# A feature-interaction kernel: who multiplies and who splits in its opening, and the order of its first weight and input loads

## The chip, the cores and the metric

The kernel runs on one core of a Trainium2 chip. The metric is the device time of one execution in microseconds (us): 2739.86 is the median of three runs (2738.73 to 2740.82). Engines: TensorE (PE), VectorE (DVE), ScalarE (ACT), GpSimd (POOL) and SyncE (SP), which here only issues DMAs.

## What is computed

1024 samples have 39 fields with an embedding of 16 numbers each. Three layers multiply every pair of rows and mix the products with a matrix; a two-layer dense net runs over the same inputs, and one dot product sums all:

```python
inputs = emb[feature_ids] * feature_vals[:, :, None]        # (1024, 39, 16)
h = inputs
for i in range(3):                                          # 200 outputs each
    x = jnp.einsum('bhd,bmd->bhmd', h, inputs).reshape(B, -1, 16)
    x = jax.nn.relu(jnp.einsum('bcd,oc->bod', x, Ws[i]) + bs[i][None, :, None])
    if i != 2:
        h, direct = x[:, :100], x[:, 100:]
    else:
        direct = x
    finals.append(direct)
cin_result = jnp.sum(jnp.concatenate(finals, axis=1), axis=-1)
d = relu(relu(inputs.reshape(B, -1) @ dnn_W0.T + dnn_b0) @ dnn_W1.T + dnn_b1)
out = concat(cin_result, d) @ fc_W.T + fc_b + sum of the input biases
```

## The kernel before

**Chunks and steps.** A chunk is one of the 16 embedding positions for 128 samples, 128 chunks in all. Step i treats layer 0 of chunk i+1, layer 1 of chunk i and layer 2 of chunk i-1, in the order of ORDER: groups P0, D0, D1, P1, D2, D3, P2, D4, D5, P3, D6, ... D11. A group is up to four tiles of 128 products x 128 samples. P0 and P1 are layer 0, P2 and P3 with D0 to D5 layer 1, P4, P5 and D6 to D11 layer 2. Products of P groups are made by GpSimd (`product`, L534) in SBUF, those of D groups by VectorE (L1112) in PSUM. Each is split in a high part (ScalarE, `high`, L833, rounded to fp32r) and a low part, what is left (`low`: GpSimd L562, VectorE L1131). PE (`multiply`, L667) multiplies high with both parts of the weights and low with the high part. Each engine works through its own list in order and waits on semaphores.

**Between the layers.** `low_copy` (ScalarE) and `evacuate` (VectorE) finish a layer's sum, `take` (ScalarE) makes h, `turn` (PE) transposes it, `spread` (ScalarE, six copies) lays it out for the products of the next layer.

**Weights.** Layer 1's and 2's go from their input to a copy in DRAM by rows (`rows_of_weights`, L309, eight DMAs in four quarters), from there to SBUF (`load_weights`, L321, 13 DMAs), and are split in five PIECES each (1600, 1600, 1600, 800 and 600 columns): the high part by ScalarE (`split_weights`, L825), the low part by VectorE (L1096). W_NEEDED names the piece that PE waits for ahead of a group. Layer 2's pieces are split within step 1, after D4 to D8 (W2_AT).

**Inputs.** 39 gathers of GpSimd (L511) fetch the first 128 samples. `first_scale` multiplies them by their values, `turn` transposes them, `store_rows` stores them to `xs` in DRAM; from there `load_layer0` (L381, 12 small DMAs) brings a chunk's layer-0 operands and `load_block` (L397) the rows `xrep` for layers 1 and 2, in four blocks e = 1, 2, 0, 3: D0 and D1 need block 1, D2 and D3 block 2, P2 and P3 block 0, D4 and D5 block 3.

**The opening.** The first two chunks' layer-0 operands don't come through DRAM: `lay_out_pairs` (L1063) copies them in SBUF, PE transposes them to PSUM (`first_inputs`, L721), `first_layer0` (L1086) copies them to SBUF on VectorE, and GpSimd multiplies and splits them. SP's list from L443 on: store the first four positions, wait, load chunk 0's blocks, copy layer 2's rows, load chunk 2's layer-0 operands, chunk 1's blocks, layer 2's weights, store the other positions. After the opening come step 1 and loops over the rest.

## Time and profile before

| | |
|---|---|
| median of three runs | 2739.86 us |
| profiled execution | 2743.04 us, its span 2740.1 us |
| busy in the span | PE 96%, VectorE 84%, ScalarE 67%, GpSimd 85% |
| DMA | 359.96 MB, mean 131 GB/s |

The span runs from the first to the last instruction. The page has it in 40 slices of 68.5 us: PE is at 0 in the first, 5 in the second, and 9 in all others but the last. The opening therefore has to be read from the timelines of the single engines.

### The profile page before, as it was taken

Reading aid. Unit: us, or ns where it says so; the run is one execution under the profiler, and the core shown is the slowest. Engines: PE = TensorE matmul, PEld = TensorE weight load, DVE = VectorE, ACT = ScalarE, POOL = GpSimd, SP = SyncE. Lnnn points to the kernel's source line nnn. Section 1 sums busy time; section 2 is a strip of 40 time slices with the busy share of each in tenths; the row PEclk is TensorE's granted clock in tenths of the full one; section 3 lists DMA queues with packets and bytes.
Section 4 is the critical chain, followed back from the end, with each engine's and each line's share of the span. In section 5 each row is a group of like instructions: output and inputs, shape, how many; then the busy total and the mean of one; then the engine's idle time right before and its main releaser. Section 6 shows DMA issues by size and latency. Waiting matters only on the chain.

```text
span 2740.1 us, 68376 instructions
## 1 busy us (share of the span) xinstructions
PE 2636.3 (96%) x17806; PEld 2626.6 (96%) x17806; DVE 2290.3 (84%) x4610; ACT 1830.4 (67%) x4776; POOL 2318.8 (85%) x2168
## 2 busy tenths in 40 slices
PE   0599999999999999999999999999999999999998
PEld 0599999999999999999999999999999999999998
DVE  3688888888888888888888888888888888888884
ACT  0566776767667767676676767777677766766763
POOL 5799888988889888898889888898888988877763
PEclk9799999999999999999999999999999999999999
DMA  8854545445444464544545445454554445445441
GB/s 149 198 135 128 137 132 136 126 120 141 130 134 132 123 151 120 138 129 122 153 117 141 126 129 146 120 141 122 142 134 124 136 122 149 129 122 140 115 127 40
DMA packets 245650, 359.96 MB, mean 131 GB/s; under 512 B 68975, under 2 KB 163026, under 8 KB 245330
## 3 DMA queue, kind: packets, MB, share of 16 engines
q1 hardware_dynamic: 231394, 352.75, 47.1%
q0 software_dynamic: 10496, 2.88, 3.0%
q10 hardware_dynamic: 3568, 2.71, 0.3%
q14 instruction: 185, 1.52, 0.2%
q8 instruction: 7, 0.11, 0.0%
HBM read 354.24 MB, written 14.17 MB: 134 GB/s over the span
## 4 chain that ended last, share of the span: by engine, by line
PE 94%; POOL 2%; SPq 2%; DVE 1%; issue 1%; DMA 1%; ACT 0%; POOLq 0%; DVEq 0%; ACTq 0%
PE acc L664 60%; PE acc L665 28%; PE acc L689 3%; POOL raw L511 1%; PE hrep L700 1%; SPq L327 0%; SPq L317 0%; DVE W L1110 0%; PE acc L764 0%; PE acc L765 0%; PE acc L766 0%; DMA odd<-lin 0%; SPq L384 0%; PE hrep L786 0%; DMA raw<-table,idx 0%
## 5 line engine op out<-in xcount | busy, mean ns | idle before, releaser
L664 PE MATMUL acc<-W,xhi_d 128*128 128x400 f32 x5632 | 1729.8, 366 | 16.8 <-DVE xhi_d L1139 6.9
L665 PE MATMUL acc<-W,xlo_d 128*128 128x200 f32 x5632 | 1438.4, 255 | 0.0
L1136 DVE TENSOR_TENSOR xlo_d<-prod_d,xhi_d 128x512 fp32r<-128x512 f32 (+1 forms) x1536 | 984.9, 641 | 191.8 <-ACT xhi_d L846 117.9
L1128 DVE TENSOR_TENSOR prod_d<-hrep,xrep 128x512 f32<-128x512 f32 (+1 forms) x1536 | 1038.7, 676 | 105.6 <-issue 33.2
L664 PEld LDWEIGHTS acc<-W,xhi_d 128*128 128x128 f32 x5632 | 1060.4, 188 | 19.8 <-DVE xlo_d L1136 8.9
L665 PEld LDWEIGHTS acc<-W,xlo_d 128*128 128x128 f32 x5632 | 1078.7, 192 | 0.0
L846 ACT ACTIVATE xhi_d<-prod_d 128x512 fp32r<-128x512 f32 (+1 forms) x1536 | 884.1, 577 | 214.6 <-PE acc L665 197.8
L570 POOL TENSOR_TENSOR xlo_p<-prod_p,xhi_p 128x512 fp32r<-128x512 f32 (+1 forms) x768 | 920.8, 1199 | 125.4 <-ACT xhi_p L840 100.8
L664 PE MATMUL acc<-W,xhi_p 128*128 128x400 f32 x2816 | 879.5, 363 | 14.9 <-POOL xlo_p L570 14.9
L559 POOL TENSOR_TENSOR prod_p<-hrep_s,xrep 128x512 f32<-128x512 f32 x512 | 666.0, 1301 | 110.3 <-ACT hrep_s L883 76.4
L665 PE MATMUL acc<-W,xlo_p 128*128 128x200 f32 x2816 | 719.3, 255 | 0.0
L840 ACT ACTIVATE xhi_p<-prod_p 128x512 fp32r<-128x512 f32 (+1 forms) x768 | 473.2, 616 | 216.5 <-PE acc L665 116.1
L664 PEld LDWEIGHTS acc<-W,xhi_p 128*128 128x128 f32 x2816 | 531.9, 189 | 16.7 <-POOL xlo_p L570 13.5
L665 PEld LDWEIGHTS acc<-W,xlo_p 128*128 128x128 f32 x2816 | 539.6, 192 | 0.0
L511 POOL DMA_INDIRECT raw<-table,idx x328 | 319.8, 975 | 110.8 <-issue 90.2
L857 ACT ACTIVATE acc_lo<-acc 128x200 f32<-128x200 f32 x384 | 130.0, 339 | 290.8 <-PE acc L665 146.3
L559 POOL TENSOR_TENSOR prod_p<-l0x 128x512 f32<-128x512 f32 x128 | 165.0, 1289 | 19.8 <-DMA l0x<-xs 19.7
L1150 DVE SCALAR_TENSOR_TENSOR spent<-acc,fcw 128x100 f32<-128x100 f32 (+1 forms) x384 | 114.0, 297 | 49.1
L1146 DVE TENSOR_TENSOR acc<-acc,acc_lo 128x200 f32<-128x200 f32 x384 | 138.9, 362 | 6.8 <-ACT acc_lo L857 6.8
L551 POOL TENSOR_TENSOR prod_p<-l0x 128x384 f32<-128x384 f32 x128 | 130.9, 1023 | 3.5 <-POOL idx L506 1.7
L865 ACT ACTIVATE hbuf<-acc 128x96 f32<-128x96 f32 x256 | 63.3, 247 | 82.3 <-DVE spent L1150 80.6
L689 PE MATMUL acc<-W,xhi_d 128*128 128x400 f32 x256 | 93.3, 364 | 0.0
(105 smaller groups left out, 1208.6 us busy)
## 6 DMA issues: line engine op xcount, KB each, us to landing
xrep<-xs SPq DMA_DIRECT2D x384, 384.0 KB
xrep<-xs SPq DMA_DIRECT2D x384, 128.0 KB
xrep<-xs SPq DMA_DIRECT2D x128, 336.0 KB
l0x<-xs SPq DMA_DIRECT2D x504, 80.0 KB
l0x<-xs SPq DMA_DIRECT2D x252, 63.0 KB
l0x<-xs SPq DMA_DIRECT2D x630, 7.0 KB
xrep<-xs SPq DMA_DIRECT2D x128, 64.0 KB
l0x<-xs SPq DMA_DIRECT2D x126, 64.0 KB
```

The costliest lines, as they stand in the source:

```text
L511: nc.gpsimd.indirect_dma_start(out=raw[:, m * EMB_COLS:(m + 1) * EMB_COLS], out_offset=None, in_=table, in_offset=bass.IndirectOffsetOnAxi ...
L551: nc.gpsimd.tensor_tensor(to, l0x[:, KT[0]:L0_SLOTS - 1, :], l0x[:, a:a + count, :], ALU.mult)
L559: nc.gpsimd.tensor_tensor(to, one.unsqueeze(1).broadcast_to([P, count, P]), many, ALU.mult).then_inc(s_prod_p, 1)
L570: nc.gpsimd.tensor_tensor(xlo_p[:, slot, 0:cols], prod_p[:, slot, 0:cols], xhi_p[:, slot, 0:cols].bitcast(F32), ALU.subtract).then_inc(s_l ...
L664: pe.matmul(bank[:, 0:2 * OUTS], hi, w, start=first, stop=last, skip_group_check=True)
L665: return pe.matmul(bank[:, 0:OUTS], lo, w[:, 0:OUTS], start=False, stop=last, skip_group_check=True)
L689: mm = pe.matmul(bank[:, 0:2 * OUTS], hi, w, start=start, stop=end, skip_group_check=True)
L840: nc.scalar.activation(xhi_p[:, slot, 0:cols], prod_p[:, slot, 0:cols], ACT.Copy).then_inc(s_hi_p, 1)
L846: nc.scalar.activation(xhi_d[:, slot, 0:cols], prod_d[d_bank(i, g)][:, 0:cols], ACT.Copy).then_inc(s_hi_d, 1)
L1128: nc.vector.tensor_tensor(to, h, xrep[:, (par + layer - 1) % 2, a:a + count, :], ALU.mult).then_inc(s_prod_d, 1)
L1136: op = nc.vector.tensor_tensor(xlo_d[:, slot, 0:split], bank[:, 0:split], xhi_d[:, slot, 0:split].bitcast(F32), ALU.subtract)
L1146: nc.vector.tensor_tensor(bank[:, 0:OUTS], bank[:, 0:OUTS], acc_lo[:, layer, :], ALU.add).then_inc(s_acc[layer], 1)
```

## The change

- `first_layer0` becomes `first_products`: VectorE copies three of the ten turned tiles to SBUF and multiplies the other seven with them in PSUM. `first_high` (ScalarE) and `first_low` (VectorE) split them. PE's `first_inputs` turns ten tiles a chunk, not eleven, in another order and into banks named `first_banks`.
- GpSimd makes no product of the first two chunks' layer 0. It makes the low parts of layer 1's pieces 0 and 1 instead (semaphore `s_wlo_p`).
- ScalarE makes the high parts of layer 1's pieces 0 and 1 ahead of the first high copies, 2 and 3 between the two chunks, 4 after them.
- VectorE's scaling and transposition of positions 4 to 15 moves behind `evacuate(0, 1)`, GpSimd's gathers behind its first products of layer 1.
- SP copies the first quarter of layer 2's rows ahead of chunk 0's blocks, and issues `load_weights(2)` before chunk 1's blocks, not after.

```diff
+        W_OF_POOL = 2
-        W_NEEDED = [{("P", 0): 1},
-                    {("D", 0): 2, ("P", 2): 3, ("D", 2): 4, ("D", 4): 5, ("D", 5): 6},
-                    {("D", 6): 7, ("P", 4): 8, ("D", 8): 9, ("D", 10): 10, ("D", 11): 11}]
+        W_NEEDED = [{("P", 0): (s_wlo, 1)},
+                    {("D", 0): (s_wlo_p, 1), ("P", 2): (s_wlo_p, 2), ("D", 2): (s_wlo, 2), ("D", 4): (s_wlo, 3),
+                     ("D", 5): (s_wlo, 4)},
+                    {("D", 6): (s_wlo, 5), ("P", 4): (s_wlo, 6), ("D", 8): (s_wlo, 7), ("D", 10): (s_wlo, 8),
+                     ("D", 11): (s_wlo, 9)}]
+        first_banks = [(acc[1], prod_d[0], prod_d[1]), (hrep[1][:].rearrange("p s n -> p (s n)"), prod_d[2], acc[2])]
+        FIRST_SLOTS = [range(KT[0], KT[0] + 3), tiles_of("P", 0), tiles_of("P", 1)]
...
             sp.wait_ge(s_xt0, 1)
             store_rows(0, 0, EARLY, s_x0)
+            rows_of_weights(sp, 2, w2, [0])
             sp.wait_ge(s_x0, 128)
             sp.wait_ge(s_wlo, W_DONE[0])
             for e in (1, 2, 0, 3):
                 load_block(0, 0, e)
-            rows_of_weights(sp, 2, w2)
+            rows_of_weights(sp, 2, w2, range(1, 4))
             sp.wait_ge(s_pt, 6)
             sp.wait_ge(s_prod_p, p_num(0, 1) + 1)
             load_layer0(2)
+            load_weights(sp, 2, w2)
             for e in (1, 2, 0, 3):
                 sp.wait_ge(s_xblk[e], BLOCK_SEM[e])
                 load_block(1, 1, e)
-            load_weights(sp, 2, w2)
             sp.wait_ge(s_xt, 1)
...
             copy_idx(1, 1)
-            pool.wait_ge(s_xin, 3)
-            gather(0)
-            product(-1, 1, 0)
-            product(-1, 1, 1)
-            low(-1, 0)
-            low(-1, 1)
-            product(0, 0, 0)
-            product(0, 0, 1)
-            low(0, 0)
-            low(0, 1)
-            for m in range(1, 4):
-                gather(m)
+            pool.wait_ge(s_pairs, 2)
+            for n, (a, b) in enumerate(PIECES[1][0:W_OF_POOL]):
+                pool.wait_ge(s_whi, W_DONE[0] + n + 1)
+                nc.gpsimd.tensor_tensor(weights(1)[:, a:b, 1, :], raw_weights(1, a, b),
+                                        weights(1)[:, a:b, 0, :].bitcast(F32), ALU.subtract).then_inc(s_wlo_p, 1)
             product(0, 0, 2)
             product(0, 0, 3)
             low(0, 2)
-            for m in range(4, 7):
+            pool.wait_ge(s_xin, 3)
+            for m in range(0, 4):
                 gather(m)
             product(1, 1, 0)
             low(0, 3)
-            for m in range(7, 9):
+            for m in range(4, 9):
                 gather(m)
...
             split_weights(0, 0)
-            high(-1, "P", 0)
-            high(-1, "P", 1)
-            high(0, "P", 0)
             split_weights(1, 0)
             split_weights(1, 1)
+            first_high(0, 0)
+            first_high(0, 1)
+            split_weights(1, 2)
+            split_weights(1, 3)
+            first_high(1, 0)
+            first_high(1, 1)
+            split_weights(1, 4)
             low_copy(0, 0, -1)
             take(0, 0)
             spread(0, 0, -1)
-            high(0, "P", 1)
-            split_weights(1, 2)
             high(0, "D", 0)
-            split_weights(1, 3)
             high(0, "D", 1)
-            split_weights(1, 4)
...
+            def first_products(c):
+                first, *banks = first_banks[c]
                 if c > 0:
                     dve.wait_ge(s_prod_p, 2 * c)
+                dve.wait_ge(s_pt, 3 * c + 1)
+                nc.vector.tensor_copy(l0x[:, KT[0]:KT[0] + 3, :].rearrange("p s n -> p (s n)"),
+                                      first[:, 0:3 * P]).then_inc(s_l0c, 1)
+                dve.wait_ge(s_l0c, c + 1)
+                for g, bank in enumerate(banks):
+                    count = len(tiles_of("P", g))
+                    to = bank[:, 0:count * P].rearrange("p (t n) -> p t n", n=P)
+                    one = l0x[:, KT[0]:KT[0] + 1, :].broadcast_to([P, count, P]) if g == 0 else l0x[:, KT[0]:KT[0] + 3, :]
+                    dve.wait_ge(s_pt, 3 * c + 2 + g)
+                    nc.vector.tensor_tensor(to, to, one, ALU.mult).then_inc(s_prod_p, 1)
+
+            def first_low(c, g):
+                n, slot, bank, cols = p_num(c - 1, g), p_slot(c - 1, g), first_banks[c][1 + g], len(tiles_of("P", g)) * P
+                dve.wait_ge(s_hi_p, n + 1)
+                if g == 1:
+                    cols -= P
+                    rows = xhi_p[:, slot, cols:cols + P]
+                    nc.vector.tensor_tensor(rows[L0_LOW:P, :], bank[L0_LOW:P, cols:cols + P],
+                                            rows[L0_LOW:P, :].bitcast(F32), ALU.subtract)
+                    nc.vector.tensor_scalar(rows[0:L0_LOW, :], rows[0:L0_LOW, :].bitcast(F32), -1.0, None, ALU.mult)
+                nc.vector.tensor_tensor(xlo_p[:, slot, 0:cols], bank[:, 0:cols],
+                                        xhi_p[:, slot, 0:cols].bitcast(F32), ALU.subtract).then_inc(s_lo_p, 1)
...
             lay_out_pairs(1)
-            first_layer0(0, (prod_d[0], prod_d[1], acc[1]))
-            first_scale(EARLY, DIM, s_xin)
-            first_biases()
-            dve.wait_ge(s_xin, 3)
-            turn(EARLY, DIM, s_xt)
-            first_layer0(1, (prod_d[2], acc[2], hrep[1][:].rearrange("p s n -> p (s n)")))
-            split_weights(1, [0, 1])
+            first_products(0)
+            first_low(0, 0)
+            first_low(0, 1)
+            first_products(1)
+            first_low(1, 0)
+            first_low(1, 1)
...
             evacuate(0, 1)
+            first_scale(EARLY, DIM, s_xin)
+            first_biases()
             product(0, 0, 5)
             low(0, 3)
+            dve.wait_ge(s_xin, 3)
+            turn(EARLY, DIM, s_xt)
             low(0, 4)
```

## Rows read from the trace of the kernel before

**Rows 1.** The page, busy time, share and count of each engine.
```profile
PE 2636.3 (96%) x17806; PEld 2626.6 (96%) x17806; DVE 2290.3 (84%) x4610; ACT 1830.4 (67%) x4776; POOL 2318.8 (85%) x2168
```
**Rows 2.** Windows: stretch, length, busy (count) by engine, granted clock, DMA share, GB/s.
```profile
100.00:120.00 20.00, 16.02 (x105) 15.16 (x104) 10.16 (x19) 9.81 (x27) 18.06 (x18) 1.00 1.03 183
120.00:140.00 20.00, 12.42 (x62) 11.55 (x63) 18.03 (x27) 13.30 (x27) 12.37 (x11) 0.74 0.60 149
140.00:2680.00 2540.00, 2534.22 (x17262) 2532.76 (x17261) 2195.25 (x4419) 1770.38 (x4658) 2202.86 (x2058) 1.00 0.50 131
```
**Rows 3.** Timeline of PE: start, duration, operation, [idle before, what ended it].
```profile
73.19 0.70 PE L664 MATMUL acc<-W,xhi_p 128*128 128x400 f32 x1 [6.07 <-POOL xlo_p L570]
...
91.03 0.70 PE L664 MATMUL acc<-W,xhi_d 128*128 128x400 f32 x1 [2.67 <-issue]
...
124.89 0.70 PE L664 MATMUL acc<-W,xhi_d 128*128 128x400 f32 x1 [6.89 <-DVE xhi_d L1139]
...
137.65 0.44 PE L664 MATMUL acc<-W,xhi_d 128*128 128x400 f32 x1 [1.78 <-DVE xlo_d L1136]
```
**Rows 4.** Timeline of SP's queue, the issues of the opening.
```profile
59.86 0.60 SPq L340 DMA_DIRECT2D odd<-lin  x1
63.41 3.43 SPq L360 DMA_DIRECT2D xs<-xt  x8
67.89 0.33 SPq L401 DMA_DIRECT2D xrep<-xs  x1
...
73.39 0.62 SPq L315 DMA_DIRECT2D lin<-w  x1
...
83.70 7.61 SPq L384 DMA_DIRECT2D l0x<-xs  x12
...
97.20 0.41 SPq L326 DMA_DIRECT2D W<-lin  x1
97.65 7.98 SPq L327 DMA_DIRECT2D odd<-lin  x1
...
113.65 7.22 SPq L360 DMA_DIRECT2D xs<-xt  x8
```
**Rows 5.** Windows while layer 2's rows, chunk 1's blocks and layer 2's weights move.
```profile
78.00:87.00 9.00, 3.05 (x10) 2.67 (x11) 4.38 (x6) 5.05 (x12) 1.56 (x4) 0.50 1.11 321
92.40:100.40 8.00, 5.01 (x20) 4.62 (x20) 7.92 (x13) 2.39 (x8) 6.76 (x6) 0.52 0.99 243
101.00:115.00 14.00, 12.02 (x81) 11.56 (x80) 8.81 (x17) 8.56 (x25) 12.87 (x14) 1.00 1.13 200
```
**Rows 6.** Timeline of ACT: splits of weights, last copy of a spread.
```profile
76.03 2.95 ACT L831 ACTIVATE W<-W 128x1600 fp32r<-128x1600 f32 x2
...
113.77 0.26 ACT L888 ACTIVATE hrep<-hrep 124x128 f32<-124x128 f32 x1
...
120.21 1.54 ACT L831 ACTIVATE W<-W 128x1600 fp32r<-128x1600 f32 x1 [4.96 <-DMA odd<-lin]
```
**Rows 7.** Timeline of DVE: splits of weights, products, the low part of D9.
```profile
90.89 4.38 DVE L1110 TENSOR_TENSOR W<-W 128x800 fp32r<-128x800 f32 x1
...
104.89 1.90 DVE L1128 TENSOR_TENSOR prod_d<-hrep,xrep 128x512 f32<-128x512 f32 x3 [2.65 <-issue]
...
121.78 1.83 DVE L1110 TENSOR_TENSOR W<-W 128x1600 fp32r<-128x1600 f32 x1 [5.81 <-ACT W L831]
...
124.87 2.46 DVE L1110 TENSOR_TENSOR W<-W 128x1600 fp32r<-128x1600 f32 x1
...
136.92 0.67 DVE L1136 TENSOR_TENSOR xlo_d<-prod_d,xhi_d 128x512 fp32r<-128x512 f32 x1
```
**Rows 8.** Timeline of POOL: its products and a low part.
```profile
69.28 1.27 POOL L559 TENSOR_TENSOR prod_p<-l0x 128x512 f32<-128x512 f32 x1
...
90.67 2.53 POOL L559 TENSOR_TENSOR prod_p<-hrep_s,xrep 128x512 f32<-128x512 f32 x2
93.17 1.25 POOL L570 TENSOR_TENSOR xlo_p<-prod_p,xhi_p 128x512 fp32r<-128x512 f32 x1
```

More of the change, by code:

```diff
@@ L217, in rec_kernel @@
         s_wlo = sem("weights_low")
+        s_wlo_p = sem("weights_low_by_gpsimd")
         s_ident = sem("ident_set")
@@ L307, in pairs, with rows_of_weights @@
                 :, c * L0_SLOTS * P:(c + 1) * L0_SLOTS * P].rearrange("p (s r) -> p s r", r=P)
-        def rows_of_weights(engine, layer, src):
+        def rows_of_weights(engine, layer, src, quarters):
             used = H_QUARTER * FIELDS
             full = used // QUARTER
-            for q in range(4):
+            for q in quarters:
                 rows = lin[layer][used * q:used * (q + 1), :]
@@ L535, in product @@
                 n, layer, tiles = p_num(i, k), layer_of("P", k), tiles_of("P", k)
-                if k < 2 and isinstance(i, int) and i < 1:
-                    pool.wait_ge(s_l0c, (i + 1) * 3 + 2 + k)
-                elif k == 0:
+                if k == 0:
                     pool.wait_ge(s_l0x, i * 192)
@@ L682, in multiply @@
                 if isinstance(i, int) and c == 0 and (kind, g) in W_NEEDED[layer]:
-                    pe.wait_ge(s_wlo, W_NEEDED[layer][(kind, g)])
+                    pe.wait_ge(*W_NEEDED[layer][(kind, g)])
                 for n, t in enumerate(tiles):
@@ L719, in step, with first_inputs @@
                         turn(1, i, i)
-            def first_inputs(c, banks):
+            def first_inputs(c):
                 pe.wait_ge(s_pairs, c + 1)
-                for n in range(L0_SLOTS):
-                    t = pe.transpose(banks[n // 4][:, n % 4 * P:(n % 4 + 1) * P], pairs(c)[:, n, :], ident[:])
-                    if n % 4 == 3 or n == L0_SLOTS - 1:
-                        t.then_inc(s_pt, 1)
+                for bank, slots in zip(first_banks[c], FIRST_SLOTS):
+                    for n, slot in enumerate(slots):
+                        t = pe.transpose(bank[:, n * P:(n + 1) * P], pairs(c)[:, slot, :], ident[:])
+                    t.then_inc(s_pt, 1)
             pe.wait_ge(s_ident, 2)
             pe.wait_ge(s_pad, 1)
-            first_inputs(0, (prod_d[0], prod_d[1], acc[1]))
-            first_inputs(1, (prod_d[2], acc[2], hrep[1][:].rearrange("p s n -> p (s n)")))
+            first_inputs(0)
+            first_inputs(1)
             multiply(-1, "P", 0)
@@ L847, in high, with first_high @@
                                          ACT.Copy).then_inc(s_hi_d, 1)
+            def first_high(c, g):
+                n, slot, cols = p_num(c - 1, g), p_slot(c - 1, g), len(tiles_of("P", g)) * P
+                act.wait_ge(s_prod_p, n + 1)
+                if some(n - (PRING - 1)):
+                    act.wait_ge(s_mm_p, n - (PRING - 1))
+                nc.scalar.activation(xhi_p[:, slot, 0:cols], first_banks[c][1 + g][:, 0:cols], ACT.Copy).then_inc(s_hi_p, 1)
             def low_copy(layer, c, i):
@@ L1079, in lay_out_pairs @@
                 for n in range(2):
-                    copy(both[:, KT[0] - 1:KT[0], n, :].rearrange("p s (j a) -> p s j a", a=A_REST),
-                         A_MAIN + L0_WHOLE, 0, 1)
-                for slot, n in ((KT[0] + 2, 0), (KT[0] + 2, 1), (KT[0] + 3, 1)):
-                    op = copy(both[:, slot:slot + 1, n, :].rearrange("p s (j a) -> p s j a", a=A_REST), A_MAIN, 0, 0)
+                    for slot, first, step in ((KT[0] - 1, A_MAIN + L0_WHOLE, 1), (KT[0] + 2, A_MAIN, 0)):
+                        op = copy(both[:, slot:slot + 1, n, :].rearrange("p s (j a) -> p s j a", a=A_REST), first, 0, step)
@@ L1084, in lay_out_pairs @@
                 op.then_inc(s_pairs, 1)
-            def first_layer0(c, banks):
+            def first_products(c):
+                first, *banks = first_banks[c]
                 if c > 0:
                     dve.wait_ge(s_prod_p, 2 * c)
-                for n, bank in enumerate(banks):
-                    count = min(4, L0_SLOTS - 4 * n)
-                    dve.wait_ge(s_pt, 3 * c + n + 1)
-                    nc.vector.tensor_copy(l0x[:, 4 * n:4 * n + count, :].rearrange("p s n -> p (s n)"),
-                                          bank[:, 0:count * P]).then_inc(s_l0c, 1)
+                dve.wait_ge(s_pt, 3 * c + 1)
[8 more added lines that the diff above has]
+                    nc.vector.tensor_tensor(to, to, one, ALU.mult).then_inc(s_prod_p, 1)
```

4 lines of the change are left out of this document (2 added, 2 removed).

## The prediction

> **What bounds the kernel now.** First the page's busy shares: TensorE (PE) is busy 2636.3 us of the span of 2740.1 us [rows 1]. Then the same by stretch: from 140 to 2680 us PE is busy 2534.22 of 2540 us at the full granted clock [rows 2]. No line that the diff touches runs there, so the change can only move the moment at which that stretch begins. In 100 to 120 us PE is busy 16.02 of 20, in 120 to 140 only 12.42 at a mean granted clock of 0.74 [rows 2]. The PE timeline gives the last holes: 6.89 us before 124.89, put down to VectorE (DVE), and 1.78 us before 137.65, which ended with VectorE's low part of group D9 of step 1. From 137.65 on PE runs without a hole [rows 3]. So this is my ruler: by how much does D9 of step 1 (137.65) move? The hole before 124.89 follows from layer 2's weights: ScalarE (ACT) waits 4.96 us for their DMA and copies the first high parts at 120.21; VectorE's first split of them runs at 121.78 [rows 6, 7]. From there to the D9 operation at 136.92 VectorE has no idle row; in its timeline this stretch is 15.1 us of work [rows 7].
>
> In front of that stands SyncE's (SP) queue. From 67.89 to 113.6 us it issues one DMA after another, in order: chunk 0's blocks, layer 2's rows (73.39), chunk 2's layer-0 inputs (83.70), chunk 1's blocks (about 91.3 to 97.2), layer 2's weights (97.20 to 113.6), stores (113.65) [rows 4]. The DMA engines were full meanwhile: share 1.11 at 321 GB/s while rows are copied, 0.99 at 243 GB/s while blocks load, 1.13 at 200 GB/s while weights load [rows 5]. Only while the small layer-0 loads are issued one by one (12 in 7.61 us from 83.70, [rows 4]) do they run dry.
>
> **Part 1: the two first chunks of layer 0.** Before, VectorE copied the turned inputs to SBUF and GpSimd (POOL) multiplied; PE's first product starts at 73.19 [rows 3]. GpSimd took 1.27 us for 128x512 at 69.28 [rows 8]; its six operations per chunk cover 1920 columns, so about 4.8 us. Now VectorE multiplies out of PSUM. The nearest row for that is its own product, 1.90 us for three 128x512, 0.63 each [rows 7]. A chunk costs it one copy, two products and the low parts: about 4 us on VectorE instead of 1.9 us of copies, and GpSimd is rid of its 4.8 us. ScalarE must now do two of layer 1's high parts (2.95 us for two, [rows 6]) before the first high copy, and for that layer 1's weights must have landed. Their last DMA is issued at 59.86 [rows 4] and ScalarE used them at 76.03 [rows 6]; the trace bounds the landing by these two. Layer 2's ended ScalarE's wait at 120.21, 6.6 us after the issue's end at 113.6; the same gives 67.1 here. Then first high copy at 70, first product on PE near 71, against 73.19. With a landing near 65 it is 69, and with the worst it is 81.
>
> **Part 2: GpSimd splits layer 1's pieces 0 and 1.** 1600 columns at 1.27 us for 512 are 3.9 us each, 7.9 us, from about 68.5 to 76.5 on an engine that has nothing else now. VectorE loses 3.9 us of splits. There is a price in the other direction: VectorE's split of 800 columns at 90.89 took 4.38 us while GpSimd ran three operations on two SBUF tensors (90.67 to 94.42), and ended 0.85 us after them [rows 7, 8]. So when both engines read two SBUF tensors VectorE stands until GpSimd has a gap. In the new opening nearly all of VectorE's operations read one operand from PSUM, as the products at 104.89 do, which show no such stretching [rows 7]; one does not, the multiplication by -1 in SBUF, which reads one SBUF tensor. No row shows such an operation beside GpSimd: 0 to 7 us.
>
> The skill states a rule for exactly this. The Trainium skill, "GPSIMD Engine Reference", section Specifications, says that GpSimd's SBUF interfaces are shared with VectorE, with contention for two SBUF inputs and for the two-port performance mode. By its second half the multiplication by -1 could stand; the trace agrees with the first half (the 4.38 us row) and has nothing on the second. By the rule the front would lose up to 7 us, by the rows alone nothing.
>
> Either way the front is early: spread of chunk 0 near 78 to 83, and PE's D0 of step 0 near 80 to 86 instead of 91.03 [rows 3]; the first scaling of inputs, now behind evacuate(0, 1), and the store of inputs (113.65) have room. What all this is worth depends on what is late next.
>
> **Part 3: the order of the DMAs.** It decides. Moving layer 2's first quarter of rows into the wait before 67.89 saves about 1.5 us of issue: the stores end at 66.84 [rows 4], a large one takes 0.62 us (73.39), I take 1.5 us for the two, so the blocks start 0.5 us later, but the engines copy rows where they were idle. The other six row DMAs end where eight did, limited by bandwidth, some 1.5 us earlier: layer-0 inputs at 82.2 instead of 83.70, done at 89.9. Then weights 2 at once, 7.3 us earlier than 97.20. Their volume is 128 x 31 rows of 800 B, 3.17 MB, at 200 GB/s [rows 5] 15.9 us: from about 91.3 on the engines to 107.2. SP is done issuing them near 104.5 (8 us after L327's wait, as from 105.7 to 113.6). Chunk 1's blocks queue behind: 128 x 31 x 512 B = 2.03 MB at 243 GB/s [rows 5] are 8.4 us, in four blocks of about 2.1: with 1 us to land, block 1 at 110.8, 2 at 112.9, 0 at 115.0, 3 with its small pieces at 117.5. Bounds for the last: 114 (the weights at the 243 GB/s of the blocks, 13 us) and 120.5 (all of it as slow as before, where the same bytes ended at 120.2).
>
> **Step 1 with late blocks.** Before, VectorE's products of chunk 1 started at 104.89, waiting for no DMA [rows 7]. Now they wait: p0 and p1 from 110.8, p2 at 112.9, low0 to 114.2, evacuate(1, 0) and low1 to 116.2. PE starts D0 at 114.2, at half clock after its pause (0.52 was the mean grant in 92.4 to 100.4, [rows 5]; a group of four tiles is eight products, at 0.7 for the first at 91.03 about 2.2 us), so D1 is done at 118.6; the transposition and ScalarE's six copies of the spread, the last of which stands at 113.77 before and which need some 1.6 us [rows 6], end at 120.8. p6 waits for that. ScalarE then has high P3 and D4, and the first split of weights 2 at 121.9; VectorE's follows at 123.4. Against 121.78 that is 1.6 us late: the wait for weights is replaced by one for blocks.
>
> From there the same 15.1 us of VectorE to D9, with one difference. Before, GpSimd idled in part of this stretch and the five splits lost little to it (the second took 2.46 us where 1.83 is normal, [rows 7]). Now GpSimd's products of step 1 start at 115 with block 0 and fall beside the splits. I take 1 us more for it, with bounds of 0 (they miss each other) and 17 us (each of five loses 3.5 us like that at 90.89: 4.38 less 0.9, half of the 1.83 for 1600 columns); 1 is nearest to what the splits of 121.78 to 136.9 show. Sum: 1.6 + 1.0 = +2.6 us on D9. The profiled execution spans 2740.1 us and took 2743.04; its span lies within 0.3 us of the median, 2739.86. The difference is applied to the median: 2739.9 + 2.6 = **2742.5 us**.
>
> **Rivals.** A change under 5.5 us (0.2%) can't be told from none here, and the cases stand on both sides of that.
> - *The stall of 6.89 us goes and the blocks are in time.* If weights and blocks move together faster than in turn, so that all blocks have landed by 106, VectorE starts chunk 1 at about 105 as before, ScalarE does the splits without a wait, and D9 comes 5.8 us earlier (VectorE's idle time before 121.78), and up to 13 us if the opening's gain survives too: 2727 to 2734. For: SP's L327 stood 7.98 us behind the backlog of blocks [rows 4], which it now would not meet. Against: the engines were full. Chance 0.08.
> - *Blocks near 114 to 116 and no collisions.* Same mechanism, small gain: 2736 to 2741. Chance 0.27.
> - *My forecast*, 2741 to 2745.3: 0.45.
> - *Slower by a collision.* GpSimd's run of products in step 1 holds VectorE's splits. It decides once three of five splits meet two GpSimd operations each (2.5 us): 3 x 2.5 + 1.6 = +9, 2749. For: the 4.38 us row, and that GpSimd has all six groups of step 1 ahead of it at 115. Against: its gathers and waits leave gaps. Chance 0.20. The Trainium skill's page above gives the rule of it ("contention with DVE instructions in a 2-port perf mode or with two SBUF inputs").
>
> **How the numbers follow.** Likeliest 2742.5. Left out below: most of the first rival; above: the collision's far end. Range 2736 to 2749.5. Faster by over 0.2% (under 2734.4): 0.08; slower by over 0.2% (over 2745.3): 0.20; within: 0.72.
>
> **What would show it.** D0 of step 0 at 80 to 86; L326 of weights 2 at 90; no wait of ScalarE for weights 2, and instead VectorE's L1128 and GpSimd's L559 waiting for `xrep<-xs` between 98 and 117; VectorE's five splits at 123 to 139, some of over 2 us; PE without holes from about 140. I am wrong if chunk 1's products start by 106, if PE's last hole ends before 134, or if the long stretch itself is no longer full.

## The result, and the profile after the change

The changed kernel takes 2756.2 us (median; 2747.6 to 2759.2 in six runs) where the kernel before takes 2739.8 us beside it (2737.1 to 2741.8, six runs). The ratio is 1.0048, with a 95% interval of 1.0038 to 1.0057: slower by some 13 us. The two medians alone lie 16.5 us apart, a little outside that interval; below I count by the ratios, as they are at hand for every kernel. The forecast, 2742.5 us with a range of 2736.0 to 2749.5, misses it.

| | before | after | after, a second trace |
|---|---|---|---|
| profiled execution, us | 2743.0 | 2751.5 | 2757.3 |
| its span, us | 2740.1 | 2749.6 | 2755.4 |
| VectorE's low part of D9 in step 1, start (the ruler) | 136.92 | 144.38 | 149.09 |

The second trace is of the same kernel, taken later. The two differ by 5.8 us, and the splits on VectorE will turn out to make most of that.

The page's first lines, and the windows that answer to [rows 1] and [rows 2] (stretch, its length, busy us and count of PE, PE's weight loads, VectorE, ScalarE and GpSimd, granted clock, DMA share, GB/s):

```profile
span 2749.6 us, 68367 instructions
PE 2637.3 (96%) x17804; PEld 2625.4 (95%) x17804; DVE 2285.2 (83%) x4613; ACT 1831.4 (67%) x4776; POOL 2320.4 (84%) x2158
100.00:120.00 20.00, 2.71 (x9) 2.36 (x10) 3.96 (x9) 2.34 (x7) 7.92 (x9) 0.50 0.94 188
120.00:140.00 20.00, 14.43 (x76) 13.46 (x76) 15.31 (x20) 13.42 (x26) 17.63 (x15) 0.87 0.36 79
140.00:2680.00 2540.00, 2533.91 (x17263) 2530.36 (x17264) 2196.13 (x4426) 1771.86 (x4660) 2207.53 (x2058) 1.00 0.49 131
```

PE's work is what it was, and the long stretch is untouched: 2533.91 us busy of 2540, before 2534.22. But between 100 and 120 us PE is busy 2.71 us instead of 16.02. PE stood there, with the DMA engines at a share of 0.94.

PE's timeline, the rows with idle time in front (start, duration, engine, line, operation, out and in, count, idle time before and what ended it):

```profile
70.74 0.70 PE L667 MATMUL acc<-W,xhi_p 128*128 128x400 f32 x1 [3.08 <-DVE xlo_p L1120]
81.79 0.45 PE L667 MATMUL acc<-W,xhi_d 128*128 128x400 f32 x1 [0.69 <-DVE xlo_d L1163]
...
106.39 0.70 PE L667 MATMUL acc<-W,xhi_p 128*128 128x400 f32 x1 [8.62 <-POOL xlo_p L579]
119.80 0.67 PE L667 MATMUL acc<-W,xhi_d 128*128 128x400 f32 x1 [10.90 <-ACT hbuf L877]
133.78 0.45 PE L667 MATMUL acc<-W,xhi_d 128*128 128x400 f32 x1 [3.29 <-DVE xhi_d L1166]
...
140.69 0.45 PE L667 MATMUL acc<-W,xhi_d 128*128 128x400 f32 x1 [1.80 <-DVE xlo_d L1163]
145.11 0.45 PE L667 MATMUL acc<-W,xhi_d 128*128 128x400 f32 x1 [0.65 <-DVE xlo_d L1163]
```

The opening does what it should: D0 of step 0 starts at 81.79 instead of 91.03 [rows 3]. Then PE waits 8.62 us for GpSimd's second layer-0 product of step 1 and 10.90 us before D0 of step 1, and its last hole, the one before D9, ends at 145.11 where it ended at 137.65. The queue of SP, and what it feeds on ScalarE, GpSimd and VectorE:

```profile
90.25 0.41 SPq L336 DMA_DIRECT2D W<-lin  x1
90.71 4.43 SPq L337 DMA_DIRECT2D odd<-lin  x1
...
104.36 0.72 SPq L411 DMA_DIRECT2D xrep<-xs  x1
109.80 0.44 SPq L426 DMA_DIRECT2D xrep<-xs  x1
```

```profile
66.52 2.96 ACT L834 ACTIVATE W<-W 128x1600 fp32r<-128x1600 f32 x2 [12.91 <-DMA odd<-lin]
127.36 1.54 ACT L834 ACTIVATE W<-W 128x1600 fp32r<-128x1600 f32 x1
```

```profile
68.21 7.14 POOL L620 TENSOR_TENSOR W<-W 128x1600 fp32r<-128x1600 f32 x2 [6.73 <-ACT W L834]
118.52 1.28 POOL L568 TENSOR_TENSOR prod_p<-hrep_s,xrep 128x512 f32<-128x512 f32 x1 [11.04 <-issue]
128.49 0.99 POOL L522 DMA_INDIRECT raw<-table,idx  x1
129.49 1.31 POOL L568 TENSOR_TENSOR prod_p<-hrep_s,xrep 128x512 f32<-128x512 f32 x1
131.52 2.11 POOL L579 TENSOR_TENSOR xlo_p<-prod_p,xhi_p 128x512 fp32r<-128x512 f32 x1 [0.71 <-ACT xhi_p L843]
```

```profile
115.68 1.30 DVE L1155 TENSOR_TENSOR prod_d<-hrep,xrep 128x512 f32<-128x512 f32 x2 [23.78 <-issue]
117.27 0.70 DVE L1155 TENSOR_TENSOR prod_d<-hrep,xrep 128x512 f32<-128x512 f32 x1 [0.29 <-DMA xrep<-xs]
126.35 0.70 DVE L1155 TENSOR_TENSOR prod_d<-hrep,xrep 128x512 f32<-128x512 f32 x1 [3.29 <-ACT hrep L899]
128.93 3.57 DVE L1137 TENSOR_TENSOR W<-W 128x1600 fp32r<-128x1600 f32 x1 [0.74 <-issue]
...
144.38 0.67 DVE L1163 TENSOR_TENSOR xlo_d<-prod_d,xhi_d 128x512 fp32r<-128x512 f32 x1
```

Layer 2's weights go out from 90.25 us and are no longer waited for: ScalarE's first high part of them at 127.36 has no idle time in front. In return VectorE stands 23.78 us for chunk 1's blocks, which land at 115.7 us, and its first split of layer 2 starts at 128.93 instead of 121.78 [rows 7]. That row takes 3.57 us instead of 1.83: GpSimd's product runs until 130.80, and only then do VectorE's 1.7 us begin; in turn GpSimd's low part at 131.52 takes 2.11 us instead of 1.28.

### The profile page after: what moved, and what is told of

Its sections match the earlier page's. It is cut to its first block, busy times and chain, and to the rows that moved or that the text cites. A ratio compares the mean times of both kernels' runs of the same rounds, so it can differ in the third digit from the quotient of the medians.

```text
span 2749.6 us, 68367 instructions
## 1 busy us (share of the span) xinstructions
PE 2637.3 (96%) x17804; PEld 2625.4 (95%) x17804; DVE 2285.2 (83%) x4613; ACT 1831.4 (67%) x4776; POOL 2320.4 (84%) x2158
## 3 DMA queue, kind: packets, MB, share of 16 engines
q10 hardware_dynamic: 3568, 2.71, 0.3%
## 4 chain that ended last, share of the span: by engine, by line
PE 92%; issue 2%; POOL 2%; DVE 2%; SPq 1%; DMA 1%; ACT 0%; DVEq 0%; ACTq 0%; POOLq 0%
PE acc L667 59%; PE acc L668 28%; PE acc L692 3%; POOL raw L522 1%; PE hrep L703 1%; DVE xlo_d L1163 1%; DMA xrep<-xs 0%; DVE W L1137 0%; DMA raw<-table,idx 0%; PE acc L767 0%; PE acc L768 0%; SPq L394 0%; PE acc L769 0%; SPq L327 0%; PE hrep L789 0%
## 5 line engine op out<-in xcount | busy, mean ns | idle before, releaser
L579 POOL TENSOR_TENSOR xlo_p<-prod_p,xhi_p 128x512 fp32r<-128x512 f32 x764 | 921.5, 1206 | 126.4 <-ACT xhi_p L843 90.6
L843 ACT ACTIVATE xhi_p<-prod_p 128x512 fp32r<-128x512 f32 x764 | 471.0, 617 | 199.4 <-PE acc L668 113.7
L568 POOL TENSOR_TENSOR prod_p<-l0x 128x512 f32<-128x512 f32 x126 | 163.2, 1295 | 15.4 <-DMA l0x<-xs 15.3
```

Of the source, the lines that this page charges most:

```text
L568: nc.gpsimd.tensor_tensor(to, one.unsqueeze(1).broadcast_to([P, count, P]), many, ALU.mult).then_inc(s_prod_p, 1)
L579: nc.gpsimd.tensor_tensor(xlo_p[:, slot, 0:cols], prod_p[:, slot, 0:cols], xhi_p[:, slot, 0:cols].bitcast(F32), ALU.subtract).then_inc(s_l ...
L843: nc.scalar.activation(xhi_p[:, slot, 0:cols], prod_p[:, slot, 0:cols], ACT.Copy).then_inc(s_hi_p, 1)
```

## The experiments

Four theories were on the table. O: the order of the DMAs alone makes the loss, and the opening's gain goes nowhere. C: PE's low clock after its pause. P: VectorE's splits collide with GpSimd. And for the 9 us won in the opening: some other engine or transfer swallows them. All ratios are to the kernel before, run beside each kernel.

**The parts apart.** First the changed kernel with the old order of DMAs (e1), and the old kernel with the new order (e2):

```
 (e1, from the changed kernel)            (e2, from the kernel before)
-            load_weights(sp, 2, w2)      +            load_weights(sp, 2, w2)
             for e in (1, 2, 0, 3):                    for e in (1, 2, 0, 3):
                 ...load_block(1, 1, e)                    ...load_block(1, 1, e)
+            load_weights(sp, 2, w2)      -            load_weights(sp, 2, w2)
```

> The changed kernel with one thing undone: layer 2's weights are issued behind chunk 1's blocks again. Theory O (the order is the whole loss): chunk 1's products start before 105 us, the wait for layer 2's weights is back and ends 1 to 2 us earlier than the 120.2 of before, because the first quarter of rows is copied in a gap; the time is 2734 to 2740 us, 0 to 5 below the kernel before. Rival R (the opening itself costs, by operations of two engines in each other's way): it stays 5 us or more above 2740.

> The kernel before with only the order changed: layer 2's weights ahead of chunk 1's blocks. Theory O: the loss is here in full, 10 to 17 us over the kernel before (2750 to 2757), with VectorE's first product of step 1 at 115 to 118 us. If the opening's other parts carry the loss instead (R), it is within 4 us of 2740.

e1: 1.0008 (0.9999 to 1.0017). e2: 1.0037 (1.0025 to 1.0049). The order is the loss in the main, with or without the new opening. Both numbers lie a little off the bands: e1 was to be 0 to 5 us below the kernel before and is some 2 above, which is not clear of zero; e2 has the 10 us that its band begins with, and its interval meets that of the changed kernel. Whether the new opening adds a microsecond or two of its own stays open. In e2 VectorE's first product of chunk 1 comes at 117.35 us and the first split at 130.19, for 3.58 us: the same picture as in the changed kernel. And in e1 the opening is early and worth nothing:

```profile
83.27 0.70 PE L667 MATMUL acc<-W,xhi_d 128*128 128x400 f32 x1 [0.60 <-DVE xlo_d L1163]
107.56 0.70 PE L667 MATMUL acc<-W,xhi_p 128*128 128x400 f32 x1 [7.93 <-POOL xlo_p L579]
124.52 0.70 PE L667 MATMUL acc<-W,xhi_d 128*128 128x400 f32 x1 [5.74 <-DVE xhi_d L1166]
```

D0 of step 0 starts at 83.27 instead of 91.03; then PE waits 7.93 us for GpSimd's second layer-0 product (1.81 us before) and 5.74 us for the split of layer 2, whose weights ScalarE takes at 119.84, against 120.21 before.

**The clock.** In the changed kernel PE comes out of its pause at a granted clock of 0.50 (1.2 GHz). e3 keeps it busy with 94 products that nobody reads:

```
             multiply(0, "P", 3)
+            filler(40)
             step(1)
...
+                    if i == 1 and (kind, g) == ("P", 0):
+                        filler(54)
```

> The changed kernel with 94 products more on PE that nobody reads (into a bank that is free then), 40 ahead of step 1 and 54 between its P0 and D0, in the time in which PE waits for chunk 1's blocks. Theory C (part of the loss, and its spread over 2748 to 2759 us, is PE resuming at half clock and staying there): granted clock 1.00 at 120 us, the transposition of h1 of chunk 0 comes some 3 us earlier than 124.3, and the time falls to 2743 to 2749 with a spread as small as before's. If the clock is not in it (the blocks' arrival alone sets the end), the time stays at 2750 to 2757.

The clock is indeed up (0.97 over 100 to 133 us, against 0.62 in the changed kernel), and VectorE's product behind the turn comes at 124.12 instead of 126.35. The time is 1.0047 (1.0033 to 1.0061), as without the filler. The 2.2 us were lost again at once: the splits then took 3.38, 3.82 and 4.63 us, and a 64x200 one 3.36. So the clock alone gives nothing back. Whether it would without the longer splits, no run shows. The splits are next.

**The collisions.** e4 is the changed kernel once more, unedited, for a second trace.

> The changed kernel once more, for a second trace: its runs lie between 2748 and 2759 us and the trace at hand is one of 2751. Theory C: if this execution is at 2755 or more, its longer time shows as more time at half clock between 100 and 170 us. If the spread is of the DMAs instead, the blocks land later than the 115.7 us of the first trace.

It took 2757.3 us. The blocks land at 116.30 instead of 115.68, ScalarE is as early, and the first split starts at the very same 128.93. From there to the low part of D9 it takes 20.2 us instead of 15.5. VectorE's rows, and GpSimd's beside the first of them:

```profile
136.52 4.63 DVE L1137 TENSOR_TENSOR W<-W 128x1600 fp32r<-128x1600 f32 x1
144.85 3.36 DVE L1134 TENSOR_TENSOR W<-odd,W 64x200 fp32r<-64x200 f32 x1
149.09 0.67 DVE L1163 TENSOR_TENSOR xlo_d<-prod_d,xhi_d 128x512 fp32r<-128x512 f32 x1
```

```profile
135.98 0.94 POOL L522 DMA_INDIRECT raw<-table,idx  x1 [0.30 <-issue]
136.95 1.29 POOL L568 TENSOR_TENSOR prod_p<-l0x 128x512 f32<-128x512 f32 x1
138.19 1.26 POOL L579 TENSOR_TENSOR xlo_p<-prod_p,xhi_p 128x512 fp32r<-128x512 f32 x1
139.62 2.39 POOL L522 DMA_INDIRECT raw<-table,idx  x1 [0.16 <-issue]
```

The split begins beside a gather of GpSimd, 0.4 us ahead of two operations that stand right behind it, and is held through both, to 139.45; its own 1.7 us end at 141.15, and now the next gather takes 2.39 us instead of 0.95. It is these two operations that hold it and not the gather. In the trace of the kernel before a split of the same size begins beside a gather that no product follows, and runs at its own length:

```profile
128.49 0.94 POOL L511 DMA_INDIRECT raw<-table,idx  x1 [0.30 <-issue]
```

```profile
129.04 1.82 DVE L1110 TENSOR_TENSOR W<-W 128x1600 fp32r<-128x1600 f32 x1
```

The same stands at 133.54 in e6 (1.82 us, gather from 133.00 to 133.94). And in e4 the first split, at 128.93, began beside a gather, 0.8 us ahead of a product: it took its 1.83 us, and the product 2.17 instead of 1.29.

From the first split to D9 VectorE has no idle row in either trace, so these rows make 4.7 of the 5.8 us between the two executions. Theory C had its sign too, a granted clock of 0.80 in 140 to 160 us against 1.00 in the first trace; it follows PE's wait of 4.32 us for VectorE, which ends at 142.40. In the first trace the splits lose only 2.1 us to GpSimd, hardly more than the 1.8 us that they lose before (124.87 and 134.18); in the second they lose 6.8. Two ways to take this away. f1 shortens layer 2's first four splits on VectorE to 200 columns, so that the rest of these low parts is left out (and f2 does so in e1):

```
+                    if layer == 2 and b < KT[layer]:
+                        src, hi, lo = src[:, 0:1, :], hi[:, 0:1, :], lo[:, 0:1, :]
```

> The changed kernel, except that VectorE takes the low parts of layer 2's first four pieces of weights for one tile of 200 columns instead of 8, 8, 8 and 4 tiles (the other low parts of layer 2 keep the raw weights, so layer 2's sums are not the reference's); every wait and every increment stands as it was. The changed kernel stood at 1.0048 of the kernel before. Theory of collisions (the two-operand splits of VectorE and GpSimd's runs of products and lows hold each other up: 3.57 us instead of 1.83 in one trace, 4.63 and 3.36 us in another): the excess goes with the splits, about 6 us, and 1 to 2 us of ordinary time with it: 1.0012 to 1.0025 of the kernel before, and the runs lie closer together than the 11 us of the changed kernel. Theory of late blocks alone (the 11 us come from chunk 1's blocks landing at 116 instead of 98, and the splits only follow): only the ordinary time of the splits that lies on the path goes, 1 to 2 us: 1.0040 to 1.0045. In both, chunk 1's first product stays at 115.5 to 116.5 us.

> The same shortened splits in the kernel with the order put back (layer 2's weights behind chunk 1's blocks), which stood at 1.0008 of the kernel before. Its splits showed no excess but 0.6 us on the second and 1.1 us on the 64x200 piece, and they follow weights that land at 119.8 us. Both theories: 0 to 3 us less than the kernel with whole splits: 0.9997 to 1.0008. The difference to the changed kernel with shortened splits tells them apart: 3 to 6 us by the theory of collisions, 10 to 12 us by that of late blocks alone (the whole kernels are 11 us apart).

f1: 1.0033 (1.0021 to 1.0046), between what the two theories gave it; the interval meets both bands. The excess had not gone with the columns. A split of 200 columns takes 0.37 us alone, and in f1:

```profile
136.19 3.23 DVE L1139 TENSOR_TENSOR W<-W 128x200 fp32r<-128x200 f32 x1
```

```profile
135.71 0.95 POOL L522 DMA_INDIRECT raw<-table,idx  x1 [0.30 <-issue]
136.67 1.30 POOL L568 TENSOR_TENSOR prod_p<-l0x 128x512 f32<-128x512 f32 x1
137.92 1.27 POOL L579 TENSOR_TENSOR xlo_p<-prod_p,xhi_p 128x512 fp32r<-128x512 f32 x1
```

What VectorE pays is GpSimd's run, here to 139.19 us, and not a share of its own work. So shortening does not help, and the test I had built on it could not separate what it was to separate. f2: 1.0011 (1.0002 to 1.0020), no better than e1 and just above its expectation, although its D9 came at 129.32 instead of 136.53. f1 and f2 stand 6 us apart, which the theory of collisions gave as 3 to 6, but with the excess still in f1 that number is no proof of it. And something else is late in f2:

```profile
139.36 0.62 PE L667 MATMUL acc<-W,xhi_p 128*128 128x400 f32 x1 [1.77 <-POOL xlo_p L579]
```

```profile
130.42 1.29 POOL L568 TENSOR_TENSOR prod_p<-l0x 128x512 f32<-128x512 f32 x1 [4.11 <-DMA l0x<-xs]
```

GpSimd waits 4.11 us for chunk 3's layer-0 inputs, which stand in SP's queue behind the weights and the stores of chunk 0's tile, and PE's last hole ends at 139.36. In e7 below it ends at 139.48, for the same engine. I read this as a floor at about the time of the kernel before, under everything that is tried here; no kernel was run with these inputs earlier. The wait could be seen in the trace of the kernel before:

```profile
132.91 1.29 POOL L559 TENSOR_TENSOR prod_p<-l0x 128x512 f32<-128x512 f32 x1 [3.48 <-DMA l0x<-xs]
```

The second way is the operand. g1 gives each split the same number of columns, but takes one operand from VectorE's own PSUM bank, so that layer 2's true low parts are left out:

```
-                    nc.vector.tensor_tensor(lo, src, hi.bitcast(F32), ALU.subtract)
+                    some_psum = prod_d[d_bank(1, d)][:, 0:HID].unsqueeze(1)
+                    nc.vector.tensor_tensor(lo..., some_psum..., hi.bitcast(F32)..., ALU.subtract)
...
+                        dve.wait_ge(s_wlo, W_DONE[2] - 2 - 4 + W2_AT[d])
```

> The changed kernel, except that VectorE's low parts of layer 2's weights subtract from a value that stands in one of VectorE's PSUM banks instead of from the raw weights in SBUF (so that layer 2's low parts are not the reference's), with a wait for its own last split behind each. The number of columns is the same. Theory of collisions (two SBUF operands on VectorE beside GpSimd's runs: 200 columns took 2.16 and 3.23 us where 0.37 is their own time; the operations with one operand in PSUM were never seen stretched): every 1600-column split takes 1.7 to 1.9 us, the 64x200 ones 0.3 to 0.5, the excess of about 6 to 8 us goes and the added waits give 0.5 to 1 back: 1.0018 to 1.0032 of the kernel before, where the changed kernel stood at 1.0048. Theory that the splits are stretched by something else (their reads beside the DMAs' or PE's): they stay at 3 to 4.6 us for some and the time at 1.0040 to 1.0055. In both the first product of chunk 1 stays at 115.5 to 117 us.

1.0026 (1.0016 to 1.0037), inside the 1.0018 to 1.0032 of theory P, and eight runs lie within 3.5 us of each other (2748.1 to 2751.6), where the changed kernel's six spread over 11.5. (That the collisions make this spread is not shown: g4 below has none and spreads over 8.4 us in eleven runs.) All 1600-column splits take 1.81 or 1.82 us, this one beside a product of GpSimd:

```profile
135.18 1.81 DVE L1139 TENSOR_TENSOR W<-prod_d,W 128x1600 fp32r<-128x1600 f32 x1
```

```profile
134.59 1.29 POOL L568 TENSOR_TENSOR prod_p<-l0x 128x512 f32<-128x512 f32 x1
```

So without collisions 0.0022 is gone, 6 us of the 13. The intervals of the two ratios leave 2 to 10 for it, and it is counted against a kernel before that has 1.8 us of collisions itself.

**The landing of the blocks.** e6 issues chunk 1's blocks between the two large and the eleven small DMAs of layer 2's weights:

```
+            def second_blocks():
+                for e in (1, 2, 0, 3):
+                    sp.wait_ge(s_xblk[e], BLOCK_SEM[e])
+                    load_block(1, 1, e)
-            load_weights(sp, 2, w2)
-            for e in (1, 2, 0, 3):
-                ...
+            load_weights(sp, 2, w2, second_blocks)    # called between large and small
```

> The changed kernel, with chunk 1's four blocks issued between the two large DMAs of layer 2's weights and the eleven small ones. Theory of the small DMAs (the weights' rows of 800 bytes went on as a trickle until 112 us; it is these small DMAs, on few partitions each, that the blocks had to share with): the blocks land 4 to 5 us earlier, first product of VectorE at 110.5 to 112 us instead of 115.7, the weights' last piece a few us later but still ahead of its split on ScalarE, and the time is 4 to 9 us below the changed kernel's: 1.0015 to 1.0033 of the kernel before. Rival (the bytes of the two large DMAs hold the blocks up, whatever lies behind them): first product at 114.5 to 116 us, time as the changed kernel's, 1.0040 to 1.0055.

1.0019 (1.0010 to 1.0028), 8 us below the changed kernel, as the theory of the small DMAs has it, and the first product came at 110.77 us:

```profile
110.77 1.30 DVE L1159 TENSOR_TENSOR prod_d<-hrep,xrep 128x512 f32<-128x512 f32 x2 [16.47 <-issue]
```

This execution ran late from its start: it issues layer 2's weights at 92.88 us, the changed kernel at 90.25, so that the hit of the forecast moment is partly luck. Counted from that issue, the first block is issued 4.7 us behind it instead of 14.1 and used 17.9 us behind it instead of 25.4; in g4 below it is 6.6 and 18.2. So the landing follows the issue. From its own issue to its first use the block needs 13.2 us here, 11.6 in g4 and 11.3 in the changed kernel, all behind the two large DMAs, and at most 4.6 in e1 (issued at 90.61, used at 95.16), where it stands ahead of the weights. The rival's time is refuted, but its thought that the large DMAs hold the blocks up is not, and nothing here speaks for a manner of the small ones beyond their place in the queue.

g4 makes both edits, that of e6 and that of g1:

> Both edits at once on the changed kernel: chunk 1's blocks issued between the large and the small DMAs of layer 2's weights, and VectorE's low parts of these weights with one operand in PSUM (so that layer 2's low parts are not the reference's). Alone they stood at 1.0019 and 1.0026 of the kernel before, where the changed kernel stood at 1.0048, and the splits of the first of the two still lost 3.5 us in its trace (2.18, 3.85 and 2.10 us for 1.83, 1.83 and 0.97). Theory of two separate causes (landing of the blocks, collisions): 3 to 4 us below the first alone, 1.0003 to 1.0010, first product of chunk 1 at 110 to 112 us, all splits at 1.8 to 1.9 us. Rival (a third wait takes over behind them, for example that for ScalarE's high parts of weights that now land later): 1.0014 to 1.0022.

1.0003 (0.9994 to 1.0012): at the edge of the band of two separate causes, with all splits at their own length. The first product came at 108.45 us, earlier than the 110 to 112 that were forecast from e6's late execution. With both edits the loss is no longer measurable: the 13 us are the blocks' late landing and the collisions, and nothing else of that size. (Alone the edits give back 8 and 6 us, together 12.3. The difference is within the intervals; the floor may take a part of it, for GpSimd waits for chunk 3's inputs in g4 too, 3.63 us until 132.36.)

```profile
108.45 1.30 DVE L1174 TENSOR_TENSOR prod_d<-hrep,xrep 128x512 f32<-128x512 f32 x2 [17.25 <-issue]
135.96 0.68 DVE L1182 TENSOR_TENSOR xlo_d<-prod_d,xhi_d 128x512 fp32r<-128x512 f32 x1
```

**Where the opening's gain goes.** Three kernels with the old order. e7 asks for layer 2's rows earlier; g2 adds to it that GpSimd's gathers stand behind its first two products of step 1; g3 adds to that that chunk 2's layer-0 inputs are loaded behind layer 2's weights:

```
 (e7, from e1)
+            rows_of_weights(sp, 2, w2, [0])
             sp.wait_ge(s_xt0, 1)
             store_rows(0, 0, EARLY, s_x0)
-            rows_of_weights(sp, 2, w2, [0])
+            rows_of_weights(sp, 2, w2, [1])
...
-            rows_of_weights(sp, 2, w2, range(1, 4))
+            rows_of_weights(sp, 2, w2, range(2, 4))
 (g2, from e7)
-            for m in range(0, 4): gather(m)
             product(1, 1, 0)
             low(0, 3)
-            for m in range(4, 9): gather(m)
-            step(1, 1, 0, range(9, BEFORE))
+            step(1, 1, 0, range(0, BEFORE))
 (g3, from g2)
-            sp.wait_ge(s_prod_p, p_num(0, 1) + 1)
-            load_layer0(2)
             for e in (1, 2, 0, 3): ...load_block(1, 1, e)
             load_weights(sp, 2, w2)
+            sp.wait_ge(s_prod_p, p_num(0, 1) + 1)
+            load_layer0(2)
```

> The kernel with the order put back, with the first quarter of layer 2's rows asked for ahead of the stores for chunk 0 and the second quarter right behind them, so that less is left between chunk 0's blocks and chunk 2's inputs. Theory (the order put back is limited by where the weights land, ScalarE's first split of layer 2 at 119.8 us with nothing else late): the weights' DMAs are issued some 3 us earlier, the split starts at 116 to 118 us, and the time falls by 1 to 4 us: 0.9994 to 1.0005 of the kernel before. Rival: the rows asked for earlier share the engines with the stores and delay chunk 0's opening (D0 of step 0 at 83.3 us now) as much as they advance the weights: 1.0005 to 1.0020.

> The kernel with the order put back and two quarters of layer 2's rows early (1.0004 of the kernel before), with GpSimd's nine gathers for the next tile that stand ahead of step 1 moved into step 1, so that its two layer-0 products of chunk 2 come at once. Where did the opening's gain of 8 to 10 us go? Theory G (GpSimd's run of gathers swallows it: PE waits 7.5 us for the second of these products, until 105.6 us): the time falls by 4 to 8 us, 0.9975 to 0.9990. Theory W (layer 2's weights land last whatever stands ahead, ScalarE's first split of them at 117 us): PE takes the second product at 97 to 100 us and then waits longer for the split of layer 2, until 121 to 122 us as before: 0.9998 to 1.0010, with up to 1 us of loss, since the moved gathers then lengthen step 1 on GpSimd.

> The kernel with the gathers moved, and with the twelve small DMAs of chunk 2's layer-0 inputs (7.6 us of SP's issue) issued behind layer 2's weights instead of ahead of chunk 1's blocks. Theory W (what bounds the opening is the DMAs in front of layer 2's weights): blocks and weights land 6 to 8 us earlier, ScalarE's first split of layer 2 starts at 109 to 112 us instead of 117, while chunk 2's first products come at 110 to 113 us, behind them: 2 to 7 us off, 0.9978 to 0.9996 of the kernel before. Rival: the products of chunk 2 come so late that PE waits for them as long as it waited for the weights: 0.9998 to 1.0020.

e7: 1.0004 (0.9995 to 1.0013), within its theory's band; the first high part of layer 2 starts at 117.10 us instead of 119.84, D9's low part at 133.69 instead of 136.53, and of these 3 us the time shows 1 at most, which fits the floor. g2: 1.0007 (0.9998 to 1.0016), theory W. Its rows:

```profile
95.22 1.01 POOL L561 TENSOR_TENSOR prod_p<-l0x 128x384 f32<-128x384 f32 x1
```

```profile
117.19 1.54 ACT L831 ACTIVATE W<-W 128x1600 fp32r<-128x1600 f32 x1 [7.20 <-DMA odd<-lin]
```

```profile
122.88 0.70 PE L664 MATMUL acc<-W,xhi_d 128*128 128x400 f32 x1 [10.18 <-DVE xhi_d L1163]
```

GpSimd's second product comes at 95.22 us instead of 102.94 in e7, and PE, no longer held by it, waits 10.18 us for the split of layer 2 instead, until 122.88 us (121.95 in e7). g3: 1.0098 (1.0084 to 1.0112), 25 us slower than g2, far outside both expectations:

```profile
107.56 9.46 SPq L394 DMA_DIRECT2D l0x<-xs  x12
```

```profile
118.49 1.26 POOL L569 TENSOR_TENSOR prod_p<-l0x 128x512 f32<-128x512 f32 x1 [31.00 <-issue]
```

The layer-0 inputs land at 118.5 us, and all of step 1 stands behind them: its first P group is what GpSimd, ScalarE's queue and PE have next, and PE waited 22.77 us for it. Layer 2's first split on VectorE came at 139.62 us, though the last of its weights was issued by 107.5. None of the variants is measurably faster than the kernel before.

## Why the prediction was wrong, step by step

| step | forecast | measured |
|---|---|---|
| layer 1's weights used by ScalarE | 67.1 | 66.52 |
| PE's first product; D0 of step 0 | 71; 80 to 86 | 70.74; 81.79 |
| multiplication by -1 beside GpSimd, extra | 0 to 7 | at least 0.6 (0.84 at 71.03, 0.23 at 75.20) |
| weights 2 first issued; all issued | 89.9; 104.5 | 90.25; 104.3 |
| **first block used** | **110.8** | **115.68** (116.30) |
| D0 of step 1 on PE | 114.2 | 119.80 |
| spread ended | 120.8 | 126.3 |
| first split of layer 2 on VectorE | 123.4 | 128.93 (128.93) |
| **split to D9, more than before's 15.1** | **+1.0** | **+0.3 (+5.0)** |
| D9 against before | +2.6 | +7.5 (+12.2) |

In brackets the second trace. What was right: the ruler, for the span followed D9 (+9.5 us of span for +7.5 of D9, and +15.3 for +12.2, the rest being mostly longer waits of PE much later); the whole front, each row within a microsecond; that the opening's gain would be hidden (e1); that the wait for weights is replaced by one for blocks; and the chain from block to split, 12.6 us forecast and 13.25 measured. The sign was right too, though I gave being measurably slower only 0.20.

What failed first is the landing of the blocks, the step "Chunk 1's blocks queue behind: 128 x 31 x 512 B = 2.03 MB at 243 GB/s [rows 5] are 8.4 us, in four blocks of about 2.1". It let weights and blocks go in turn, and had the first block in use 6.3 us after its issue; it took 11.3. The windows of the changed kernel show 181 GB/s in 90 to 100 us, 200 in 100 to 110 and 238 in 110 to 115.7. At these rates the same sum gives 108.0 for the weights and 2.6 us for the first block, 111.6 with the microsecond to land: the rates explain 0.8 us. The other 4 I put down to the assumption of turns, which the bytes speak against. From 90 to 115.7 us the engines moved 201 GB/s x 25.7 us = 5.2 MB, and weights and first block together are 3.7: the other 1.5 MB belonged to what was queued around them, the rest of the layer-0 inputs, the other three blocks (all issued by 110.2), the stores behind them and gathers. No trace shows which of them went ahead of the first block. The bounds I gave were for the last block alone, 114 to 120.5; the first, on which the step hangs, had none. That is the step that failed: a term with no bounds, where all four blocks in flight together would have said up to 117.

The second is the size of the collisions. The mechanism, its row and its place were in the prediction, as a term of 1 us and a rival of 7.5 at 0.20. In the first trace the term of 1 us was even too large (+0.3, for +7.5 of D9 in all), in the second it was +5.0, and removing it gave back 6 us (g1). My bound of 17 held; my choice in it was the row nearest in time, where GpSimd was idle in part, though the step before had just put GpSimd's whole run of step 1 beside the splits. I had also missed a row of the kernel before, where the splits lost 1.8 us and not only the 0.6 that I named:

```profile
134.18 1.49 DVE L1105 TENSOR_TENSOR W<-W 64x200 fp32r<-64x200 f32 x1
```

And I treated the two as alternatives, though nothing keeps them apart: the blocks can be late and the splits held as well. 2742.5 + 4.9 for the blocks + 6.5 for a rival of 7.5 in place of 1.0 is 2753.9, near the measured median of 2756.2 and a microsecond above what the ratio gives. That late blocks bring on the collisions, by starting GpSimd's run late, is not shown: in e6, with blocks in use earlier, the splits still lost 3.5 us, more than in the changed kernel's first trace.

The rival of a vanished stall (2727 to 2734) would not have come true even with blocks in time, as far as f2 and e7 show: D9 came 7.6 and 3.2 us earlier than in the kernel before, PE waited for GpSimd until 139.4 instead, and the time did not fall. I had named no such floor, because I asked what was late at 137 and not what would be late next.

## What to carry to other kernels

When a queue is reordered, the transfer that is moved back needs bounds for its first piece, with everything in flight counted against it, because its consumer waits for the first piece. A delay also moves the engines against each other: ask which pairs of operations it brings side by side, and price these at the length of the neighbour's run. And before a stall is counted as a gain, take the next transfer in the same queue and see when that would have to land.

## What the runs showed of the hardware

VectorE's tensor_tensor with two SBUF operands, begun while a tensor_tensor of GpSimd runs, is held until GpSimd's run of them ends and then runs at its own length: 3.82 us for 1600 columns in e3, 1.83 alone. It was held too when it began beside a gather, 0.4 to 0.6 us ahead of such a run: 4.63 us for 1600 columns, 3.36 for 64x200 (0.36 alone), 3.23 for 200 columns (0.37 alone). A gather with nothing behind it held no split (1.82 us at 129.04 before and at 133.54 in e6). GpSimd is held in the same way: gathers begun during a split took 2.39 us instead of 0.95, its low part 2.11 instead of 1.28. With one operand in PSUM nothing of it is seen (1.81 and 1.82 us). One operation with a single SBUF operand met GpSimd as well: the multiplication by -1 took 0.84 us at 71.03 and 0.23 at 75.20. In e1, where it took 0.83 from 72.36 on, it ended 0.12 us after GpSimd had passed from the first to the second of its own two operations (at 73.07).

The Trainium skill, "SBUF — State Buffer", section "Who interferes with whom", has the rule: a VectorE instruction with two SBUF inputs contends with a GpSimd one that reads SBUF, and one with at most one SBUF input, outside the two-port modes, does not. The traces agree with both: e4's split took 4.63 us, g1's 1.82 at most. Of the two-port modes the same section says that who issues first has the ports "for the whole instruction". On the length of a hold the traces of two SBUF operands go beyond that: the split at 136.52 us was held not for one instruction of GpSimd but through two that followed each other without a gap, until 139.45, though it had started before both.

PE's granted clock stayed at 0.95 in 100 to 120 us with unread products between its groups, against 0.50 without (of the two levels, 2.4 and 1.2 GHz, 0.50 is the lower); that brought the product behind the turn of step 1 forward by 2.2 us and the kernel's end by nothing.
